# Batch norm, two group norms and two convolution stacks: separate stages, or one pipeline of 48 strips

## The reference

```
x = x + attention(group_norm(x))          # L0: windows, 8 heads
x = x + relu(batch_norm(conv3x3_grouped(group_norm(x))))   # L1: 32 groups, statistics over all images
x = x + stack2(group_norm(x))             # L2
x = x + stack3(group_norm(x))             # L3, as L2 with other weights

def stack(x):                             # in-place updates of channel slices
    A = x
    for i in range(4):   A[..., 32*i:32*i+32] = A @ w1 + b1
    A = relu(A)
    for i in range(4):   A[..., 32*i:32*i+32] = conv3x3(A, w2) + b2
    A = relu(A)
    for i in range(128): A[..., i] = A @ w3 + b3
    return A + x
```

## Time and profile before

| | us |
|---|---|
| median of 3 runs | 2451.2 (2449.58 to 2453.36) |
| profiled execution | 2451.15 |
| its span | 2449.3 |
| PE busy | 2036.9 (83%) |
| DVE busy | 1683.8 (69%) |
| ACT busy | 1168.9 (48%) |
| POOL busy | 1079.8 (44%) |

### The profile page before, as it was taken

The page is one execution under the profiler, slowest core; times in us unless marked ns, Lnnn a source line. Parts: engine busy times, 40 slices in busy tenths (PEclk is TensorE's granted clock), DMA queues, the critical chain, the costliest instruction groups (busy, mean ns, idle before and its releaser), DMA issues. The chain is left out here.

```text
span 2449.3 us, 74821 instructions
## 1 busy us (share of the span) xinstructions
PE 2036.9 (83%) x30446; PEld 1076.8 (44%) x30446; DVE 1683.8 (69%) x3438; ACT 1168.9 (48%) x2597; POOL 1079.8 (44%) x1227
## 2 busy tenths in 40 slices
PE   6699889988998899859992049999996499999996
PEld 5455555555555555535551013444442133333332
DVE  4589999999899989942225955666664455566553
ACT  6576667666676667622223414444432044333330
POOL 0377777776777777759304723222210131111100
PEclk8899999999999999969996569999999599999997
DMA  8300000000000000002225931444434224444444
GB/s 230 102 24 24 21 21 22 24 21 19 24 22 21 21 24 21 21 10 90 99 98 221 393 131 50 134 133 142 140 110 140 92 62 107 127 126 127 118 99 109
DMA packets 240572, 215.47 MB, mean 88 GB/s; under 512 B 123248, under 2 KB 228464, under 8 KB 238192
## 3 DMA queue, kind: packets, MB, share of 16 engines
q1 hardware_dynamic: 240240, 210.77, 28.3%
HBM read 78.29 MB, written 75.50 MB: 63 GB/s over the span
## 5 line engine op out<-in xcount | busy, mean ns | idle before, releaser
L1181 POOL TENSOR_SCALAR l_x<-l_x,l_scale,l_shift 128x384 f32<-128x384 f32 x192 | 155.4, 810 | 600.5 <-PE banks L1408 600.5
L423 POOL TENSOR_TENSOR at_prob<-at_prob,at_inv 128x512 f32<-128x512 f32 x288 | 294.2, 1042 | 116.6 <-DVE at_inv L563 111.4
L489 ACT ACTIVATE at_prob<-at_prob 128x512 f32<-128x512 f32 x288 | 181.9, 632 | 306.2 <-DVE at_prob L553 306.2
L1371 PE MATMUL banks<-l_a,l_taps 128*32 128x384 f32 x3456 | 310.9, 490 | 8.4 <-ACT l_r L1231 8.4
L1386 PE MATMUL banks<-l_above,l_taps 128*32 128x384 f32 x1728 | 310.2, 492 | 2.8 <-ACT l_above L1245 1.8
L1386 PE MATMUL banks<-l_below,l_taps 128*32 128x384 f32 x1728 | 308.9, 492 | 0.0
L605 PE MATMUL banks<-at_xn,at_w 128*64 128x256 f32 x2336 | 286.0, 387 | 1.8 <-ACT at_xn L441 1.4
L1241 ACT ACTIVATE l_above<-l_below 96x384 f32<-96x384 f32 x144 | 75.5, 524 | 414.8 <-DVE l_below L1314 414.8
L1314 DVE SCALAR_TENSOR_TENSOR l_below<-banks,l_b,l_old 128x384 f32<-128x384 f32 x144 | 89.0, 618 | 217.7 <-PE banks L1386 187.7
L1300 DVE COPY l_old<-l_a 32x384 f32<-32x384 f32 x576 | 208.4, 362 | 26.1 <-ACT l_a L1218 14.9
L644 PE MATMUL banks<-const,at_prob 128*128 128x128 f32 x1152 | 184.0, 287 | 50.1 <-POOL at_prob L423 47.1
(11 more groups left out here) (142 smaller groups left out, 3616.4 us busy)
## 6 DMA issues: line engine op xcount, KB each, us to landing
l_x<-x_mid SPq DMA_DIRECT2D x48, 768.0 KB, 4.4
l_rows<-l_r SPq DMA_DIRECT2D x768, 48.0 KB, 2.0
at_k_bd<-at_k SPq DMA_DIRECT2D x584, 32.0 KB, 1.8
load_raw<-in_x SPq DMA_DIRECT2D x36, 512.0 KB, 4.8
y<-c_y SPq DMA_DIRECT2D x96, 192.0 KB
bn_y<-y SPq DMA_DIRECT2D x8, 2304.0 KB, 11.0
x_mid<-x_res SPq DMA_DIRECT2D x8, 2304.0 KB, 15.6
x_mid<-l_x SPq DMA_DIRECT2D x24, 768.0 KB, 3.7
```

The lines of the kernel that those rows point to most:

```text
L423: nc.gpsimd.tensor_tensor(prob[i][p][:, :, :], prob[i][p][:, :, :], inv[i][p][:, :].unsqueeze(2).broadcast_to([P, HEADS, WIN]), ALU.mult). ...
L489: nc.scalar.activation(prob[j % 2][p][:, :, :], prob[j % 2][p][:, :, :], ACT.Exp).then_inc(s["exped"], 1)
L1371: last = nc.tensor.matmul(grid(acc(k)[block_rows(c), :]), e[:, dy + 1, dx, :], a[:, k % A_RING, rows_, dx:dx + SIDE], start=(dy, dx) == TA ...
```

## The change

What it does, in words:

- **x is stored during attention.** x_dram is one half of a DRAM tensor `both`, y the other. SP stores the finished tiles of a row of blocks at the last step of the next row (`store_x`), 28 DMAs in all, and waits for them at the end. This x isn't centred, so nothing uncentres it later.
- **Stack weights are prepared inside the grouped convolution.** The chain of both stacks is cut into ten pieces (`Prepared`), one in each even group from 2 to 20: PE's piece in the middle of the group's taps, DVE's before that group's statistics.
- **batch_norm_stage and both pairs of group norm and stack become tail_stage**, one pipeline of 48 strips (24 of each stack, `kind` 0 and 1) with `steps = range(-2, strips + 6)`. Ahead of it stand the batch statistics, then the first image in 12 half strips of 768 tokens ("units"): SP loads x straight into its ring and y into `work`; ACT applies ReLU, DVE adds (POOL each third), DVE takes statistics. Then the norm of the first image.
- **The other three images** come through `work` as 36 units inside the steps, three in each of steps -2 to 1 and two in each of steps 2 to 13: SP loads x and y of a unit in one DMA, ACT applies ReLU, POOL adds, DVE takes two statistics, SP stores x; the strip is loaded again by its step.
- **The other seven norms** run inside the stream, each for one image of one stack, cut in five parts on DVE and three products on PE; they start at steps 2, 8, 12, 14, 18, 24 and 30.

The core of the diff:

```diff
@@ attention_stage, SP
+            def store_x(row):
+                sp.wait_ge(s["added"], row.number * 4 + 1)
+                t = row.tile_before(0)
+                run = 3 if row.r == 0 else 4
+                for t, run in ((t, run), (row.tile_before(3), 1))[:5 - run]:
+                    at = slice(t * TILE, (t + run) * TILE)
+                    sp.dma_start(x_dram[:, at], sh.x[:, at]).then_inc(s["x_stored"], 16)
             def step(n, j, row):
                 spread(n + 2, j % 2)
+                if j == ROW_STEPS - 1 and not row.first:
+                    store_x(row)
...
+            sp.wait_ge(s["x_stored"], 16 * (B * ROW_STEPS + B))
@@ conv1_stage, PE and DVE
+                if g and prepare_at(g - 1) is not None:
+                    pe.wait_ge(prepared.by_dve, prepare_at(g - 1) + 1)
                 for n, (dy, dx) in enumerate(taps):
+                    if n == len(taps) // 2 and prepare_at(g) is not None:
+                        pe.wait_ge(s["y_kept"], 4 * g)
+                        prepared.on_tensor(pe, prepare_at(g))
...
+                if prepare_at(g) is not None:
+                    prepared.on_vector(dve, link, prepare_at(g))
-def batch_norm_stage(sh, gb_dram, y_dram, x_dram):
...
-def stack_stage(sh, tag, w_dram, x_dram, out_dram=None):
+def tail_stage(sh, w_drams, prepared, gb_dram, both_dram, out_dram):
...
+        norms = [((0, 0), None), ((0, 1), 2), ((0, 2), 8), ((1, 0), 12), ((0, 3), 14), ((1, 1), 18), ((1, 2), 24), ((1, 3), 30)]
...
+        work_places = [(k, p) for k in range(-2, 2) for p in range(3)]
+        work_places += [(k, p) for k in range(2, 2 + IMG_STRIPS * (B - 2)) for p in range(2)]
@@ tail_stage, SP
+            for k in range(IMG_STRIPS):
+                sp.dma_start(x[:, k, :], x_dram[:, k * STRIP:(k + 1) * STRIP]).then_inc(first_in[k], 16)
+                if k < WORK_UNITS:
+                    first_y(2 * k)
+                    first_y(2 * k + 1)
...
+            def work_load(n):
+                if n < works:
+                    i, use = n % WORK_UNITS, n // WORK_UNITS
+                    if use:
+                        sp.wait_ge(work_out[i], 16 * use)
+                        sp.wait_ge(s["counted_w"], HALF_TILES * (n - WORK_UNITS + 1))
...
+                    sp.dma_start(work[:, work_slot(n), :], both_dram[:, :, unit_columns(FIRST_UNITS + n)])\
+                        .then_inc(work_in[i], 16)
+            def work_store(n):
+                sp.wait_ge(s["added_w"], n + 1)
+                sp.dma_start(x_dram[:, unit_columns(FIRST_UNITS + n)], work_x(n)).then_inc(work_out[n % WORK_UNITS], 16)
+            def work_move(k, p):
+                if (k, p) in work_at:
+                    n = work_at[k, p]
+                    if n:
+                        work_store(n - 1)
+                    if n + 1 >= WORK_UNITS:
+                        work_load(n + 1)
...
             for k in steps:
+                work_move(k, 0)
                 turn(k - 5, 3)
                 if k >= 0:
                     load(k + 2)
-                for q in (1, 0, 2):
-                    turn(k - 4, q)
+                turn(k - 4, 1)
+                turn(k - 4, 0)
+                work_move(k, 1)
+                turn(k - 4, 2)
                 store(k - 6)
+                work_move(k, 2)
@@ tail_stage, POOL
                     scale_x(STRIP_T * k + p + TILE_LEAD)
+                    work_add(k, p)
@@ tail_stage, ACT
                 spread(k - 2, 1)
                 keep_a(at + TILE_LEAD)
                 keep_r(k - 2, 1)
+                work_relu(k, 0)
                 keep_a(at + TILE_LEAD + 1)
                 spread(k - 3, 2)
                 keep_a(at + TILE_LEAD + 2)
                 keep_r(k - 3, 2)
+                work_relu(k, 1)
                 spread(k, 0)
+                if k in norm_at:
+                    norm_root(norm_at[k])
                 keep_r(k, 0)
                 keep_r(k - 4, 3)
                 keep_a(at + TILE_LEAD + 3)
+                work_relu(k, 2)
@@ tail_stage, DVE (norm_a to norm_e of the seven norms, not shown, stand between these)
                 update(at + 1)
                 keep_out(at)
+                work_count(k, 0)
                 find_delta(k - 3, 2)
                 keep_old(k, 1, (2, 3))
                 shift_below(k - 3, 2)
                 update(at + 2)
                 keep_out(at + 1)
+                work_count(k, 1)
                 keep_old(k, 2, (0, 1))
                 find_delta(k, 0)
@@ tail_stage, PE
                 dense(k, 0)
                 fold(k - 2, 0)
+                if k - 1 in norm_at:
+                    norm_bias(norm_at[k - 1], at)
                 mix(at)
                 dense(k, 1)
+                if k in norm_at:
+                    norm_mean(norm_at[k], at + 1)
                 mix(at + 1)
                 fold(k - 3, 1)
+                if k in norm_at:
+                    norm_var(norm_at[k], at + 2)
                 mix(at + 2)
```

More of the change, by code:

```diff
@@ L702, with prepare_at @@
+PREPARES = 10
+def prepare_at(g):
+    return g // 2 - 1 if g % 2 == 0 and 0 < g <= 2 * PREPARES else None
 C1_T = 4
@@ L1083, in stack_stage, with kind_of, column, image @@
+        ps_y_mean, ps_y_total = sh.bank[0][:, 0:4], sh.bank[1][:, 0:2]
+        gavg = sh.const[:, C_GAVG:C_GAVG + P]
         inner = slice(1, 1 + SIDE)
+        def kind_of(k):
+            return k // per_kind
+        def column(k):
+            return k // IMG_STRIPS
+        def image(k):
+            return slice(column(k), column(k) + 1)
+        norms = [((0, 0), None), ((0, 1), 2), ((0, 2), 8), ((1, 0), 12), ((0, 3), 14), ((1, 1), 18), ((1, 2), 24), ((1, 3), 30)]
+        norm_at = {start: n for n, (_, start) in enumerate(norms)}
@@ L1131, in load @@
             def load(k):
-                if has(k):
+                if has(k) and k >= IMG_STRIPS:
+                    n = k - IMG_STRIPS
                     if k >= X_RING:
                         sp.wait_ge(x_out[(k - X_RING) % 2], 16 * ((k - X_RING) // 2 + 1))
+                    if kind_of(k):
+                        sp.wait_ge(x_out[k % 2], 16 * ((k - per_kind) // 2 + 1))
+                    else:
+                        for unit in (2 * k - FIRST_UNITS, 2 * k + 1 - FIRST_UNITS):
+                            sp.wait_ge(work_out[unit % WORK_UNITS], 16 * (unit // WORK_UNITS + 1))
@@ L1351, in _, with norm_product, norm_mean, norm_var @@
                 keep_out(at + 2)
+                work_count(k, 2)
+                if k in norm_at:
+                    norm_d(norm_at[k])
         @block.tensor
         def _(pe):
-            pe.wait_ge(s["taps_in"], 16)
+            pe.wait_ge(s["chain"], 5)
+            nc.tensor.matmul(ps_y_mean, sh.const[:, C_SAME:C_SAME + P], y_mean[:, :], start=True,
+                             stop=True).then_inc(s["y_averaged"], 1)
+            pe.wait_ge(s["chain"], 9)
+            for r_ in range(4):
+                at = C_OWN + P - QUARTER - QUARTER * r_
+                last = nc.tensor.matmul(ps_y_total, sh.const[:, at:at + P], y_both[:, r_, :], start=r_ == 0,
+                                        stop=r_ == 3)
+            last.then_inc(s["y_averaged"], 1)
+            def norm_product(n, phase, out, lhs, rhs, at):
+                pe.wait_ge(s["gn_dve"], 4 * n + (1, 2, 4)[phase])
+                wait(pe, s["gn_read"], 3 * n + phase)
+                wait(pe, s["out_kept"], at - TURN_LAG - 1 - kind_tiles)
+                nc.tensor.matmul(out, lhs, rhs, start=True, stop=True).then_inc(s["gn_pe"], 1)
+            def norm_mean(n, at):
+                norm_product(n, 0, ps_mean, gavg, t3[:, :], at)
+            def norm_var(n, at):
+                norm_product(n, 1, ps_var, gavg, t2[:, :], at)
+            def norm_bias(n, at):
+                kind, b, of = norm_columns(n)
+                norm_product(n, 2, ps_bias, m1[:, kind, :], gshift[:, of], at)
+            norm_mean(0, 0)
+            norm_var(0, 0)
+            norm_bias(0, 0)
+            def read_before(at):
+                n = len(norms) - 1
+                step, p = at // STRIP_T, at % STRIP_T
+                done = 0
+                if (step, p) >= (norms[n][1], 1):
+                    done = 1
+                if (step, p) >= (norms[n][1], 2):
+                    done = 2
+                if (step, p) >= (norms[n][1] + 1, 0):
+                    done = 3
+                return 3 * n + done
             def dense(k, part):
```

558 lines of the change are left out of this document (319 added, 239 removed).

## The result

Four runs of the changed kernel took 2430.26 to 2433.68 us, median 2431.15; four of the kernel before beside them 2449.58 to 2453.36, median 2450.94. The ratio is 0.992, with an interval of 0.991 to 0.993: 0.8% faster. The forecast was 2332 (2290 to 2392), so the direction was right and the size wrong by 99 us.

What follows compares the result with a forecast made beforehand. PE was taken to bound attention and the middle of both stacks, but to stand mostly idle before the tail and partly between stacks. Gains 168.3 less costs 49.5, net 118.8, took 2451.15 to 2332 us (2290 to 2392).

Steps and rivals of the forecast that it cites:

- Gain 1: Start of the tail: 132.0 us from first batch norm instruction to first stack product become 43.1, 88.9 saved.
- Gain 2: Between the two stacks: one pipeline removes drain, group norm, preparation and refill, 77.6 us saved.
- cost 1: Attention: 28 stores of x on SP, hidden inside the stage, the last pair waited for; 4 us (3 to 5).
- cost 2: Grouped convolution: ten small PE pieces in mid-group, 6 us (2 to 15).
- Cost 5: Steps 2 to 13, two units each: 5.9 us of VectorE time against 5.6 spare, plus norms; 12 us (0 to 40).
- rival of the bound chain: Work steps: ReLU, POOL addition and count bound them, 72 us instead of 12, total 2392; 12 in 100.
- two causes offered for steps above 19 us: Work steps: chain or late turned rows, told apart by what PE's row product waits for; 12 in 100 each.
- Cost 3: Fill, steps -2 to 1: three units in each, 4.0 us a unit, lengthen it by 10 us (0 to 20).
- the earlier eviction: Start of the stack: grid clearing on DVE no longer holds ScalarE's first eviction, 1.8 us saved.
- Cost 4: Seven norms in the stream: three lone PE products and a wait for DVE each, 16 us (7 to 28).
- The low clock: Fill: PE stays at the low clock because of holes, +10 us, total 2342; 6 in 100.
- Contention: Work steps: GpSimd's additions slow VectorE, 1.0 us a step; at its strongest cost 5 would grow by 36 us.

Runs made afterwards that it cites:

- run 12: Kernel before, with four more statistics of a constant tile on VectorE in each of the first stack's 24 steps; 2477.4 us, from 2454.9.
- run 5: Changed kernel, each unit counted one place later on VectorE and a strip's fourth ReLU moved ahead of the unit's second ReLU on ScalarE; 2340.7 us.
- Run 2: Changed kernel without any of the 36 units of images 1 to 3, those of the fill included; 2316.2 us.
- run 3: Changed kernel, VectorE counting each unit one place later, the last of an image ahead of its norm; 2403.9 us.
- runs 8 and 10: Changed kernel with later count and earlier fourth ReLU, plus a ring of four units: 2340.4 us; the second also requests units one place earlier: 2338.9 us.
- run 7: Changed kernel with one group norm instead of eight, every strip using the first image's scales and biases; 2399.6 us.
- run 9: Changed kernel with 18 products of two constants on PE ahead of the first dense product of steps 5 to 14; 2407.8 us.
- run 4: Changed kernel, a strip's fourth ReLU moved on ScalarE ahead of spread and another ReLU, still behind the unit's ReLU; 2371.2 us.

## Why the prediction was wrong

**Gain 1** held: 43.4 us for 43.1. **Gain 2** held: no gap at step 24, and steps 14 to 29 at 18.26 us carry the norms. **Costs 1 and 2** with the semaphore clearing were 11.5; the tail started 8.8 later. The trace tells them apart: attention takes 978 us in both kernels, and from its last product to the convolution's first 18.9 us became 21.7, so cost 1 was some 3 us instead of 4. The convolution, from its first product to its last, took 203.1 us before and 208.8 after, but 202.8 to 208.8 in the twelve executions with the pieces, and 206.1 in run 12, which has none: the 6 us of cost 2 are not clear of that movement.

**Cost 5 failed**, by some 56 us in steps 5 to 14 alone (69.8, where its 1 us a step and the norms of steps 8 and 12 gave 13.6). The failed step is "5.9, against 5.6 spare": the busy share of VectorE, 11.8 of 17.4 us, was taken for time that can be filled. What it added up first was about right: 5.9 us a step, of them 2.7 of wait for the second addition, where 3.1 were measured for both (28.1 in nine steps); 5.6 us a step went into the loop and 2.1 into the clock. It was the subtraction that failed, though the prediction had named its condition ("The spare holds only while the waits don't line up"). Run 12 refutes it in the kernel before. The sum followed the late count to "the copies of old a and the next delta, for which ScalarE's spread and PE's folds wait", and stopped there; it didn't ask what else stands behind that spread on ScalarE. It was `keep_r(k - 4, 3)`, for which PE's next dense product waits, and the row that says how much room was left (6.0 us, 16 times, 0.5 at most) was in the trace and not used. The rival of the bound chain was right in kind. That its 72 us is close to the 69.8 is partly luck: it counted 6.0 us in each of twelve steps, the nine steps lost 7.7 each, 2.1 of that by the clock, which it didn't carry. It had 12 in 100 and was worked out from VectorE's time alone. Of the two causes offered for steps above 19 us, the row product's missing wait decides for the chain, as the prediction said it would. With the loop cut (run 5) two units a step cost 0.8 us, about the 1 us that was forecast: the estimate describes a kernel in which the order lets the spare time be used.

**Cost 3 failed**: the fill grew by 44.7 us where costs 3 to 5, less the earlier eviction, gave 13.5. Run 2 puts 41.4 of it on the units, run 3 gives 16.9 back with the count alone. "4.0 a unit" took the ring's round of load, ReLU and addition for the limit. VectorE's in-order wait for the additions was the larger part that was found; the ring and the place of the request were worth 9 us (runs 8 and 10, both cuts in place), and what makes up the last 17 stays open.

**Cost 4 was mis-sized**: 27 us for 16, just under the upper bound of 28. The three products are short; the waits beside them at steps 30 and 31, where the transposes share their bank, were not in the sum, nor was the loop, which VectorE's part of a norm seems to lengthen (no run shows that directly). Steps 14 to 29 and the rest, +25.5 us together, are mostly this: 21.9 by run 7.

**The low clock** was a rival for the fill and came true there and in the work steps. In the fill the granted clock was 0.77 on average instead of 0.91, and PE was busy 79.0 us instead of 65.9 with about as many products (726 and 736 recorded): 13 us more, where the rival took 10; how much of it was paid no run shows. In the work steps the clock fell to the lower level, 1.2 GHz, in the wait of 5.6 us and was back at 1.00 in the third of these windows (changed kernel):

```profile
1602.00:1604.00 2.00, 1.37 (x12) 0.58 (x16) 0.55 (x1) 0.95 (x3) 0.27 (x1) 0.58 1.00 402
1604.00:1606.00 2.00, 2.00 (x20) 0.70 (x16) 0.00 (x0) 0.00 (x0) 0.00 (x0) 0.56 1.02 375
1606.00:1608.00 2.00, 2.00 (x28) 0.82 (x24) 0.00 (x0) 0.00 (x0) 0.00 (x0) 1.00 1.14 240
```

Trainium skill, TensorE: Matmul & The Clock Gate (HAM oscillation): an engine left idle between bursts falls back to half rate; the trace agrees, 3.67 us for a product that takes 2.13 at 1.00, and run 9 prices it at 2.1 us a step.

**Contention** was weighed and is there. Trainium skill, GPSIMD Engine Reference (Specifications): GpSimd shares its SBUF interfaces with VectorE and contends with those of VectorE's instructions that have two SBUF inputs or run in a two-port mode. The trace agrees in part: the copies, which have one input, take 444 ns beside full additions and 354 beside small ones; in which mode they run no row shows. The 36 us that the rule at its strongest would have added were not seen: the changed kernel's copies lost 10.7 us in nine steps, and with the loop cut the run with small additions gives 3.6.

**Misses by stretch.** Start -2.4, fill +31, steps 5 to 14 +56, steps 14 to 29 +6, the rest +10: together 101 us, the miss of the profiled execution, which took 2.5 us more than the median. The fill's is explained but for 17 us.

## What to carry to other kernels

Idle time of an engine isn't spare time when engines run in order: before work is added to a queue, follow every instruction behind it to the engine that waits for it, until the loop closes or ends, and look for even a tenth of a microsecond of wait at its end, for that says that little slack is left. Taking out a semaphore wait need not cut the link: look whether the next instruction meets the same work in another way, as the copies of run 3 did. A wait for another engine belongs one place later than its data's arrival, and an instruction that frees a buffer belongs ahead of anything that must wait; here two such moves, with no work removed, were worth 85 to 90 us of 2431 (2340.7 against 2431.2; 0.957 of the kernel before against 0.992). If a summed cost is far from its measurement, the order of one queue is the first thing to move.

## What the hardware showed that I had not expected

A copy on VectorE that meets an addition on GpSimd can stand still until it ends. Timeline of run 4, two pairs of the same copy, the second beside an addition:

```profile
1600.08 0.72 DVE L1474 COPY l_old<-l_a 32x384 f32<-32x384 f32 x2
...
1602.02 2.25 DVE L1474 COPY l_old<-l_a 32x384 f32<-32x384 f32 x2
...
1602.04 2.02 POOL L1220 TENSOR_TENSOR l_work<-l_work 128x768 f32<-128x768 f32 x1 [2.30 <-ACT l_work L1273]
```

The pair takes 2.25 us instead of 0.72 and ends 0.2 us after the addition. The mean over a stretch, 444 against 354 ns, hides that it is all or nothing. Instruction by instruction, twelve of these copies overlap an addition in the nine steps of run 4: four began before it and kept their 350 ns, eight met it running and ended 0.2 us after it. In run 3 this took back about half of what the late count had saved VectorE.

And PE was faster with more to do: 18 useless products in its wait kept the clock at 1.00 and took 19 us off nine steps.
